# Two chained attention blocks on eight images: a new order for the first two images, a re-dealt steady turn, and splits moved from VectorE to GpSimd

## The reference

```
# layer 0, per image; q, k have 32 channels, v has 256
q = Wq x + bq ; k = Wk x + bk ; v = Wv x + bv
x = gamma * v softmax(q^T k)^T + x

# layer 1, per image
h = group_norm(x, 32 groups of 8 channels) * w + b
q = q_w h + q_b ; k = k_w h + k_b ; v = v_w h + v_b         # 256 channels each
y = x + proj_w (v softmax(q^T k / sqrt(256))^T) + proj_b
```

## Time and profile before

| what | value |
|---|---|
| median of 3 runs | 894.11 us |
| the profiled execution's own time | 895.79 us |
| its span, first to last instruction | 894.0 us |
| TensorE busy | 815.5 us, 91% of the span |
| VectorE busy | 555.5 us, 62% |
| ScalarE busy | 480.8 us, 54% |
| GpSimd busy | 130.8 us, 15% |
| TensorE's mean granted clock | 0.956 of 2.4 GHz |

### The profile page before, as it was taken

How to read it: one execution, slowest core, us unless ns; L and a number is a source line. 1 busy time by engine, 2 the same in 40 slices (tenths; PEclk the granted TensorE clock), 3 DMA queues, 4 the chain that set the end, 5 groups by cost and what they waited for, 6 DMA issues and landing times.

```text
span 894.0 us, 9612 instructions
## 1 busy us (share of the span) xinstructions
PE 815.5 (91%) x3756; PEld 658.4 (74%) x3756; DVE 555.5 (62%) x795; ACT 480.8 (54%) x623; POOL 130.8 (15%) x117
## 2 busy tenths in 40 slices
PE   5679779797899998999899998999899998999898
PEld 4458658685678776888678876788678786887686
DVE  6555554575756766585755857576755856465655
ACT  4745554443764476554765556654755545444243
POOL 1300030102121032100231032100222002100200
PEclk9769889899999999999999999999999998999999
DMA  6000010000110002000110002000010001000101
GB/s 212 1 0 1 1 47 1 1 0 1 47 48 1 1 1 95 1 1 1 47 49 0 1 1 88 8 0 1 1 48 1 1 1 48 1 1 1 48 1 47
DMA packets 10364, 18.96 MB, mean 21 GB/s; under 512 B 2128, under 2 KB 3920, under 8 KB 10320
## 3 DMA queue, kind: packets, MB, share of 16 engines
q1 hardware_dynamic: 10320, 18.36, 6.0%
HBM read 9.97 MB, written 8.39 MB: 21 GB/s over the span
## 4 chain that ended last, share of the span: by engine, by line
PE 67%; DVE 21%; ACT 8%; issue 2%; DMA 0%; POOL 0%; SPq 0%; ACTq 0%; DVEq 0%; POOLq 0%
PE ring L432 21%; PE ring L433 20%; PE ring L434 20%; DVE neg_raw L828 3%; PE ring L441 3%; ACT prob L633 2%; PE ring L449 2%; DVE pt_lo L846 2%; DVE x L876 2%; DVE bn L886 2%; DVE pt_lo L843 2%; DVE neg_max L826 2%; ACT ring L654 1%; DVE h_f L746 1%; DVE v_lo L810 1%
## 5 line engine op out<-in xcount | busy, mean ns | idle before, releaser
L432 PE MATMUL ring<-pt_hi,v_hi 128*128 128x512 f32 x512 | 207.8, 406 | 10.9 <-POOL v_lo L402 5.4
L433 PE MATMUL ring<-pt_lo,v_hi 128*128 128x512 f32 x512 | 204.8, 400 | 0.0
L434 PE MATMUL ring<-pt_hi,v_lo 128*128 128x512 f32 x512 | 204.5, 399 | 0.0
L633 ACT ACTIVATE prob<-ring,neg_max 128x1024 f32<-128x1024 f32 x64 | 71.5, 1117 | 191.2 <-DVE neg_max L829 191.2
L828 DVE TENSOR_REDUCE neg_raw<-ring 128x1 f32<-128x1024 f32 x64 | 77.9, 1217 | 109.3 <-PE ring L434 109.3
L432 PEld LDWEIGHTS ring<-pt_hi,v_hi 128*128 128x128 f32 x512 | 99.4, 194 | 35.7 <-DVE pt_lo L846 6.4
L434 PEld LDWEIGHTS ring<-pt_hi,v_lo 128*128 128x128 f32 x512 | 98.9, 193 | 22.5
L843 DVE TENSOR_TENSOR pt_lo<-prob,pt_hi 128x1024 fp32r<-128x1024 f32 x64 | 79.2, 1246 | 55.9 <-ACT pt_hi L644 55.8
L433 PEld LDWEIGHTS ring<-pt_lo,v_hi 128*128 128x128 f32 x512 | 99.4, 194 | 19.2
L432 PE MATMUL ring<-h_hi,query_hi 128*128 128x512 f32 x256 | 103.7, 405 | 10.2 <-ACT ring L654 4.9
L826 DVE TENSOR_REDUCE neg_max<-ring 128x1 f32<-128x1024 f32 x64 | 77.8, 1222 | 53.4 <-PE ring L441 53.2
(11 more groups left out here) (114 smaller groups left out, 1231.8 us busy)
## 6 DMA issues: line engine op xcount, KB each, us to landing
out_y<-res SPq DMA_DIRECT2D x32, 256.0 KB, 2.3
x_in<-in_x SPq DMA_DIRECT2D x7, 1024.0 KB, 4.9
x_in<-in_x SPq DMA_DIRECT2D x2, 512.0 KB, 4.9
h_f<-in_wv_t SPq DMA_DIRECT2D x1, 256.0 KB, 5.2
res<-in_wq SPq DMA_DIRECT2D x1, 256.0 KB, 7.1
res<-in_wk SPq DMA_DIRECT2D x1, 256.0 KB, 7.3
res<-in_wv SPq DMA_DIRECT2D x1, 256.0 KB, 7.6
res<-in_wp_t SPq DMA_DIRECT2D x1, 256.0 KB, 7.5
```

The lines of the kernel that those rows point to most:

```text
L432: mm(out, w_hi, m_hi, start=first, stop=False)
L433: mm(out, w_hi, m_lo, start=False, stop=False)
L434: return mm(out, w_lo, m_hi, start=False, stop=last)
L633: activation(prob[:, p % PROBS], ring[:, slot], ACT.Exp, bias=neg_max[:, k % 2:k % 2 + 1], accum_out=row_sum[:, k % 2:k % 2 + 1]).then_inc ...
```

## The change

- `head`, `turn(0)` and `turn(1)` are replaced by `first_image` and `second_image`. In the first image the weight products come one by one between the scores, the keys start without scores beside them, and most scores and value projections of image 1 follow inside the first values phase. Tiles may be given a fixed slot (`PLACE`); a step can use slots 2 and 3 as long as no phase holds them.
- In a steady turn the first qk tile moves from step 1 to step 0, the last four scores tiles from steps 8 to 11 to steps 8, 9, 11 and 12, the first value projections from step 10 to step 9 (none in step 10), the statistics from step 10 to 11, ScalarE's `h_hi` from step 15 to step 1 of the next turn.
- h in full and `h_lo` go to GpSimd (for images 0 and 7 half of the `h_lo` stays on VectorE), and so do the splits of the layer-0 value weights, of the weight products, of image 2's x, the two small memsets and the bias rows. ScalarE copies the weight products out of PSUM.
- The rounded key rows that ScalarE made (L683) are made by VectorE now, so a qk tile costs two ScalarE instructions and three VectorE ones, before three and two.
- VectorE handles the lo part of logits tile 6 before the row maximum of tile 7, and values wait for two value tiles at a time instead of all.

The core of the diff:

```diff
+PLACE = {("qk", 1, 0): 0, ("qk", 1, 1): 3}
+PLACE.update({("weights", 0, m): 3 for m in range(4)})
+PLACE.update({("value1", i, m): m for i in (0, IMAGES - 1) for m in (2, 3)})
+X_LO_ON_DVE = (0,)
+H_LO_ON_DVE = (0, IMAGES - 1)
...
+def first_image():
...
+    for m, k in enumerate((5, 6, 7)):
+        steps[2].late += tiles("weights", 0, (m,)) + tiles("scores", 0, (k,))
...
+        step = Step(("keys", 0, k) if k < TILES else None, (0, 0, k - 2) if k >= 2 else None, 1)
...
+def second_image():
...
+    s3.statistics = 0
...
+    e8.banks_first = 4
+    e8.sides = tiles("query", 0, (0,))
+    e8.late = tiles("scores", 2, (2,))
...
 def turn(i):
...
+    steps[2].banks_first = 0
+    if has(i + 1):
+        steps[0].sides = tiles("qk", i + 1, (0,))
+        steps[2].sides = tiles("qk", i + 1, (1,))
+        for k, s in enumerate((4, 5, 6, 7)):
+            steps[s].early = tiles("scores", i + 1, (k,))
+        for k, s in enumerate((8, 9, 11, 12)):
+            steps[s].late = tiles("scores", i + 1, (4 + k,))
+        for m, s in enumerate((9, 11, 12, 13)):
+            steps[s].sides = tiles("value0", i + 1, (m,))
+        steps[12].log = steps[13].shifts = i + 1
+        steps[14].sides = tiles("shift", i + 1, (0,))
+    if has(i - 1):
+        for m, s in enumerate((3, 4)):
+            steps[s].sides = tiles("query", i - 1, (m,))
+        for m, s in enumerate((5, 6, 7, 8)):
+            steps[s].sides = tiles("value1", i - 1, (m,))
+        steps[1].hidden = i - 1
+    if i == IMAGES:
+        steps[0].hidden, steps[1].hidden = i - 1, None
+        steps[7].sides = []
+        for m, s in ((2, 8), (3, 9)):
+            steps[s].sides = []
+            steps[s].late = tiles("value1", i - 1, (m,))
+    if has(i):
+        steps[11].statistics = i
+        for m, s in enumerate((12, 13)):
+            steps[s].late = tiles("norm", i, (m,)) + steps[s].late
+    if has(i + 2):
+        steps[14].split_x = i + 2
     return steps
...
+        _slot = PLACE.get(_entry, min(_step.slots, key=_given.get))
+        SLOT[_entry], BEFORE[_entry] = _slot, _last.get(_slot)
...
+            sp.wait_ge(S["x_split"], 2)
...
+            def hidden(i):
+                if i - 1 in H_LO_ON_DVE:
+                    pool.wait_ge(S["h_split"], CT * i)
+                for ct in range(CT):
+                    G.tensor_scalar(h_f[:, ct], x1[:, ct], norm_a[:, ct:ct + 1], norm_c[:, ct:ct + 1],
+                                    ALU.mult, ALU.add).then_inc(S["h_full"], 1)
             def split_hidden(i):
-                for n in range(4):
-                    ct, cols = n // 2, half_cols[n % 2]
-                    link(G.tensor_scalar(h_f[:, n % 2], x1[:, ct, cols], norm_a[:, ct:ct + 1],
-                                         norm_c[:, ct:ct + 1], ALU.mult, ALU.add))
-                    if n % 2 == 0:
-                        pool.wait_ge(S["h_hi"], 2 * i + ct + 1)
-                    last = G.tensor_tensor(h_lo[:, ct, cols], h_f[:, n % 2], h_hi[:, ct, cols].bitcast(F32),
-                                           ALU.subtract)
-                last.then_inc(S["h_split"], 1)
+                for ct in range(1 if i in H_LO_ON_DVE else CT):
+                    pool.wait_ge(S["h_full"], CT * i + ct + 1)
+                    pool.wait_ge(S["h_hi"], CT * i + ct + 1)
+                    G.tensor_tensor(h_lo[:, ct], h_f[:, ct], h_hi[:, ct].bitcast(F32),
+                                    ALU.subtract).then_inc(S["h_split"], 1)
...
+            def small_things():
+                for j in range(2):
+                    G.memset(k4[j][96:98].bitcast(F32), 1.0).then_inc(S["small_ready"], 1)
+                    pool.wait_ge(S["small_ready"], j + 1)
+                pool.wait_ge(S["wv0_loaded"], 16 * 4)
+                link(G.tensor_copy(wv0_hi[:], wv0_f))
+                G.tensor_tensor(wv0_lo[:], wv0_f, wv0_hi[:].bitcast(F32), ALU.subtract).then_inc(S["v0_weights"], 1)
+                G.tensor_copy(ident_r[:], ident_s[:]).then_inc(S["small_ready"], 1)
+                link(G.tensor_scalar(gbv[:], bv0_s[:], gamma_s[:], None, ALU.mult))
+            def bias_rows():
+                pool.wait_ge(S["weights_loaded"], 16 * 11)
+                for rows, b in ((bv_rows, bv_s), (bq_rows, bq_s)):
+                    for ct in range(CT):
+                        G.tensor_scalar(rows[:, ct], ones[:], b[:, ct:ct + 1], None,
+                                        ALU.mult).then_inc(S["rows_ready"], 1)
+            def split_weights():
+                pool.wait_ge(S["weights_read"], 2)
+                for hi, lo, src in ((wqq_hi[:], wqq_lo[:], wqq_f), (wpv_hi[:, :, 0:C], wpv_lo[:, :, 0:C], wpv_f)):
+                    link(G.tensor_copy(hi, src))
+                    G.tensor_tensor(lo, src, hi.bitcast(F32), ALU.subtract).then_inc(S["weights_split"], 1)
-            pool.wait_ge(S["bias_ready"], 1)
+            small_things()
+            pool.wait_ge(S["x0_loaded"], 16)
+            pool.wait_ge(x_loaded[0], x_loads(0))
             residual0(0)
             first_split_x()
+            bias_rows()
+            split_weights()
+            split_x(2)
             for i in range(IMAGES):
                 coefficients(i)
-                if i + 2 < IMAGES and i + 2 not in X_LO_ON_DVE:
+                if i == 0:
+                    pool.wait_ge(S["weights_split"], 2)
+                hidden(i)
+                if 0 < i < IMAGES - 2:
                     split_x(i + 2)
-                if i not in H_LO_ON_DVE:
-                    split_hidden(i)
+                split_hidden(i)
...
-                if k == 0 and 0 in banks:
-                    wait(("value0_split", "value1_split")[layer], 4 * i + 4)
+                if k % 2 == 0 and 0 in banks:
+                    wait(("value0_split", "value1_split")[layer], 4 * i + k // 2 + 1)
...
                     act.wait_ge(S["ring_ready"], RING_NO[entry] + 1)
                     q, k, cols = q4[i % 2], k4[i % 2], half_cols[m]
-                    activation(q[0:64, cols], out[0:64, 0:HALF], ACT.Identity, bias=bqk_s[0:64])
-                    activation(k[0:32, cols], out[64:96, 0:HALF], ACT.Identity, bias=bqk_s[64:96])
+                    activation(q[0:64, cols], out[0:64, 0:HALF], ACT.Identity,
+                               bias=bqk_s[0:64]).then_inc(S["qk_hi"], 1)
                     activation(k[64:96, cols], out[96:128, 0:HALF], ACT.Identity,
-                               bias=bqk_s[96:128]).then_inc(S["qk_hi"], 1)
+                               bias=bqk_s[96:128]).then_inc(S["key_hi"], 1)
+            def take_weights():
+                act.wait_ge(S["ring_ready"], RING_NO["weights", 0, 3] + 1)
+                wqq_ps, wpv_ps = weight_places(SLOT["weights", 0, 3])
+                activation(wqq_f, wqq_ps, ACT.Identity, scale=C ** -0.5).then_inc(S["weights_read"], 1)
+                copy(wpv_f, wpv_ps).then_inc(S["weights_read"], 1)
...
-                f = h_f[:].rearrange("p s n -> p (s n)")
-                for ct in range(CT):
-                    dve.wait_ge(S["h_hi"], 2 * i + ct + 1)
-                    link(V.tensor_scalar(f, x1[:, ct], norm_a[:, ct:ct + 1], norm_c[:, ct:ct + 1], ALU.mult, ALU.add))
-                    if ct == 0:
-                        link(V.tensor_tensor(h_lo[:, ct], f, h_hi[:, ct].bitcast(F32), ALU.subtract))
-                    else:
-                        V.tensor_tensor(h_lo[:, ct], f, h_hi[:, ct].bitcast(F32), ALU.subtract).then_inc(S["h_split"], 1)
+                ct = CT - 1
+                dve.wait_ge(S["h_full"], CT * i + ct + 1)
+                dve.wait_ge(S["h_hi"], CT * i + ct + 1)
+                V.tensor_tensor(h_lo[:, ct], h_f[:, ct], h_hi[:, ct].bitcast(F32),
+                                ALU.subtract).then_inc(S["h_split"], 1)
...
+                    q, k, cols = q4[i % 2], k4[i % 2], half_cols[m]
+                    link(V.tensor_scalar(k[0:32, cols], out[64:96, 0:HALF], bqk_s[64:96], None, ALU.add))
+                    V.scalar_tensor_tensor(k[32:64, cols], out[64:96, 0:HALF], bk0_s[:],
+                                           k[0:32, cols].bitcast(F32), ALU.add, ALU.subtract)
                     dve.wait_ge(S["qk_hi"], 2 * i + m + 1)
-                    q, k, cols = q4[i % 2], k4[i % 2], half_cols[m]
                     V.scalar_tensor_tensor(q[64:96, cols], out[0:32, 0:HALF], bqk_s[0:32],
-                                           q[0:32, cols].bitcast(F32), ALU.add, ALU.subtract)
-                    V.scalar_tensor_tensor(k[32:64, cols], out[64:96, 0:HALF], bk0_s[:],
-                                           k[0:32, cols].bitcast(F32), ALU.add,
+                                           q[0:32, cols].bitcast(F32), ALU.add,
                                            ALU.subtract).then_inc(S["qk_split"], 1)
...
-                if now.log is not None:
-                    shifts(now.log)
                 if now.evacuate:
                     evacuate(*now.evacuate)
```

(16 more changed lines are left out.)

263 lines of the change are left out of this document (124 added, 139 removed).

## The result

The changed kernel takes 861.8 us (median of 4 runs, 860.7 to 870.6), the kernel before 893.9 in the same comparison: a ratio of 0.966 (95% interval 0.962 to 0.970). The forecast was 847 with 828 to 870. The profiled execution has a span of 860.7 us against 894.0, so 33.3 us went. The forecast wanted 47.5.

A forecast was written before the change was run, and what follows sets the result against it. TensorE's work was put at 743 us for eight images, the rest of 894 being waits and lowered clock. Gains 12 + 1 + 3.5 + 1 + 11 + 5 + 6 + 8 = 47.5 gave 847 us, range 828 to 870.

The forecast's parts named there:

- rival B: GpSimd's new queue meets VectorE: turns 2 to 6 gain nothing, first images half; 875 us, chance 0.16.
- its own sign: Forecast is wrong if a turn takes over 102 or under 97 us, or the first two images end after 212.
- First image: New order of weight products, scores and values in image 0 gains 11 us, bounds 4 and 16.
- Passage: From image 0 to 1, a shorter chain behind the last values tile gains 5 us, bounds 0 and 8.
- Logits of image 0: Norm tiles take an already read tile's slot, statistics come five steps earlier: 8 us gained, bounds 3 and 10.
- Turns 3 to 6: h and h_lo off VectorE, qk tile a step earlier: 3.0 us gained a turn, 12.0 for four turns.
- Removed 5.7: Waits and half clock at each turn's boundary, some 5.7 us a turn, go with the change.
- Turn 7: Evacuation no longer waits behind h_lo on VectorE: 3.5 us gained, bounds 1 and 5.8.
- Re-dealt steps: Scores, value projections and statistics moved in steps 4 to 14: from -1 to +1.5 us a turn, taken as 0.
- A: Rival: waits really go, first images as short as TensorE allows, boundary costs nothing; 818 us, chance 0.19.
- C: Rival: slower, as h_lo behind x_lo on GpSimd ends after the query tile could start; 916 us, chance 0.04.
- D: Rival: waits only change their name at the query tile and image passages; 893 us, no difference, chance 0.03.

The follow-up runs named there:

- e7 (a): e1 with image 1's second statistics product ahead of scores row 7 at logits tile 5; run with a second edit moving value projections: 836.1 us, 0.935.
- e9: e1 plus e7 (a), with the shift product of image 2 right behind logits tile 7 and its copy before that tile's exponent: 833.0 us, 0.933.
- e2: Changed kernel with GpSimd's h_lo subtraction cut to 8 columns in images 1 to 6: 847.7 us, 0.949.
- e4: Changed kernel with the old deal of scores, layer-0 value projections and statistics: 863.9 us, 0.968.
- e3: Kernel before with only h_lo of images 1 to 6 moved from VectorE to GpSimd, which recomputes h in halves: 893.4 us, 1.001.
- e6: Kernel of e3 with ScalarE's h_hi of images 1 to 6 moved from step 15 to the next turn's step 1: 912.0 us, 1.020.
- e1: Changed kernel with VectorE reading the second qk tile before the lo part of keys tile 2 in turns 2 to 6: 837.8 us, 0.938.

## Why the prediction was right, and where it was not

The median lies in the stated range, in the part that the range took in from rival B and not in the forecast's own 836 to 860. By its own sign the forecast was wrong where it named the turns: turns 2, 3 and 4 take over 102 us. That the time stayed inside the stated range is owed to its width and not to the turns.

The time lost in a stretch is counted here as its length less its matmuls at 0.228 us (512 columns; 128 columns a quarter of it) and 0.119 (256), in both traces.

- **First image, 11.** Lost up to keys tile 0 of image 1: 46.1 before, 35.3 after: 10.8 (both with 9 us of waiting for the first image). The second values tile starts at 52.2, forecast 54. The stretch behind it has no idle time and a clock of 0.93, before 0.94.
- **Passage, 5, and image 1, 6.** 10.6 to 6.3 and 17.7 to 12.4: 4.3 and 5.4, near the forecast and inside its bounds.
- **Logits of image 0, 8.** 12.0 to 6.5: 5.5. What is missing lies at logits tile 6, which waits 2.1 us for the exponent of scores row 7 and runs at half clock after it (1.7); the forecast gave the norm tiles' slot and overlooked who comes behind them. e7 (a) and e9 won it back.
- **Turns 3 to 6, 12, and turn 2, 1: the step that failed.** Removed 5.7 is right: the trace of before loses 5.9 at the boundary, and 0.1 of it is left in steps 0 to 2. The new wait was put at 1.6 with 1.1 for lo parts beside `h_lo`, 2.7 together; it measured 3.3, made of 1.7 for the order (e2) and 1.55 for the one lo part that stands ahead of the read. `h_lo` was put at 14.0 from the turn's start and ended at 13.6. What the sum left out is the half clock behind the new wait: 2.5 us in turns 2, 3 and 4, 1.5 in turn 6, 0 in turn 5. The forecast had charged the old wait for its clock (2.0 of the 4.6) and not the new one. The check is turn 5, which waited 3.2 and kept its clock: 100.0 us, forecast 99.4. The others took 101.5 to 102.7. Turns 3 to 6 brought 3.4 us in place of 12.
- **Turn 2** had lost less before and now loses like the rest: +3.2 in place of -1.
- **Turn 7, 3.5, and the end, 1.** 4.8, inside its bounds, and 2.1, just past its upper one.
- **Re-dealt steps, 0.** e4: 0.
- **The cause of the 5.7.** The forecast put it down to h and `h_lo` in VectorE's queue, on the earlier trace rows. e3 takes them off that queue and the wait stays; e6 moves `h_hi` as well, and 3.4 of the 5.9 go. VectorE only stood busy while it would have waited for ScalarE's qk rounding. The other 2.5 go in the changed kernel with the earlier qk tile and its one ScalarE instruction less, which no run takes apart. That the 5.7 was right is luck in part: the change moved all of these at once. `h_hi` at the later step with `h_lo` left on VectorE was not run.
- **The rivals.** A (818) needs no wait at the boundary: e1 shows that this was there to be had, by the order of two entries, and e9 (833.0) comes to about the half way of A, 832. B had the turns right (0.3 us gained in 2 to 6) for half the right reason: a lo part does wait for a GpSimd instruction, but the query tiles do not wait for `h_lo`. C came true in e6 only. D holds for the turns taken alone (12.7 us of waiting gone, 16.2 come). The time lay between the forecast and B.
- **The exclusion of the two engines.** The forecast read the lo part of 2.14 as losing to x_lo "only in part". The rule of the Trainium skill, "SBUF — State Buffer", section "Who interferes with whom", agrees with these rows once the remainder is counted, not the length. The lo part of 418.13 met the second `h_lo`, which ended at 419.8: 1.7 left of it, and 1.2 of its own, 2.9 for a measured 2.77. The one of the earlier trace rows came 1.35 us into the first of two x_lo that started at 426.76. The row joins the two; if the first is taken at 2.36, as when alone, 1.0 of it was left: 1.0 and 1.2, 2.2 for 2.14. The cast of the earlier trace rows, 0.17 us at its other places, has one input in SBUF and so is not the form that the prediction names; it waited all the same, from 220.84 to the end of the second x_lo at 223.10, 2.26 for a measured 2.29.

Open stays why the clock falls behind one wait of 3.2 us and not behind the next. The runs show only how often. The changed kernel's other runs spread from 859 to 869 us of span at clocks from 0.976 to 0.959, the longer ones at the lower clock, so part of its time is most likely this difference in the clock; e1's clock was 0.984 to 0.986, with 835.9 to 838.1 over four runs.

## What to carry to other kernels

Price a new wait with the clock behind it: here 3.3 us of idle TensorE cost up to 5.8, 1.7 mostly cost 1.7, and the four turns that differ only in this took 100.0 to 102.5 us. When work leaves an engine's queue, ask what that engine would have waited for instead: VectorE's 4.1 us hid a wait for ScalarE, and taking them away alone brought nothing (e3). In a queue in order, the read that frees a slot goes ahead of work whose result is wanted later; here that was 9 us later (a start at 406.85 possible in e1, TensorE at 415.64), and the swap was worth 24 us.

## What the runs showed of the hardware

- VectorE's lo part (two inputs in SBUF) takes 1.23 us alone (the median of the 64 of L923 in the kernel after) and 2.8 to 2.9 in the seven that meet an `x_lo` or `h_lo` of GpSimd. VectorE's instructions that read PSUM keep their time beside it: the four-bank evacuation 2.48 us beside `h_lo`, the qk reads 0.74 to 0.75.
- GpSimd pays too: the two residual copies behind `h_lo` took 3.17 us where two alone take 2.4, and 4.3 in e1, where they meet two of VectorE's lo parts.
- Behind equal waits of 3.2 to 3.3 us the query tile took 5.29, 5.29, 5.28, 2.90 and 4.45 us in the kernel after, and 5.29, 5.29, 2.90, 4.45 and 4.07 in e4; behind waits of 1.65 to 1.71 (e2) it took 2.90 four times and 4.45 once.
